# One kernel for an adaLN block: the first batch, the last batch and the written order changed

## The reference

```python
mod = (silu(c) @ wmod).reshape(16, 6, 1, 128)          # sa, ca, ga, sb, cb, gb
ga, gb = (2*(g >= 0) - 1) * maximum(abs(g), 0.25)      # for g = ga, gb
h = layernorm(x) * (1 + ca) + sa
x = x + ga * attn(h)
h = layernorm(x) * (1 + cb) + sb
x = x + gb * moe(h)

# attn: q, k, v = h @ W.T + b, 16 heads of 8
q = softmax(q, channels of a head); k = softmax(k, tokens)
state = k^T v (per head);  o = q state
o = (o - mean) * rsqrt(var + eps) * ln_g + ln_b;  return o @ Wo.T + bo

# moe: 8 experts, top 2 of softmax(h @ router_w), weights not renormalised
y = sum_e prob_e * (gelu(h @ w_in[e] + b_in[e]) @ w_out[e] + b_out[e])
```

## Time and profile before

| | us |
|---|---|
| median of 3 runs | 373.28 (373.12 to 373.51) |
| the profiled execution | 374.83 |
| its span on the core | 373.0 |

### The profile page before, as it was taken

How to read it: one execution, slowest core, us unless ns; L and a number is a source line. 1 busy time by engine, 2 the same in 40 slices (tenths; PEclk the granted TensorE clock), 3 DMA queues, 4 the chain that set the end, 5 groups by cost and what they waited for, 6 DMA issues and landing times.

```text
span 373.0 us, 8255 instructions
## 1 busy us (share of the span) xinstructions
PE 354.6 (95%) x2532; PEld 321.6 (86%) x2532; DVE 287.4 (77%) x1060; ACT 306.3 (82%) x524; POOL 227.8 (61%) x221
## 2 busy tenths in 40 slices
PE   2987999999999999999999999999999999999995
PEld 2766878899999989999999889999999989987984
DVE  3798888987897867787896888888886968656652
ACT  3567898999899899899998999899978968885740
POOL 3256947495649766583838658494758856184561
PEclk9999999999999999999999999999999999999999
DMA  5156055352607152241607035350606060416390
GB/s 171 32 147 228 0 167 203 116 173 47 223 20 228 55 181 105 114 168 52 236 3 255 31 114 171 113 173 25 232 5 226 2 206 24 175 54 175 141 304 36
DMA packets 18962, 47.84 MB, mean 128 GB/s; under 512 B 2587, under 2 KB 6118, under 8 KB 18662
## 3 DMA queue, kind: packets, MB, share of 16 engines
q1 hardware_dynamic: 18432, 46.77, 38.0%
...
## 4 chain that ended last, share of the span: by engine, by line
PE 69%; issue 8%; DVE 6%; ACT 6%; DMA 5%; POOL 4%; SPq 0%; ACTq 0%; POOLq 0%; DVEq 0%
PE pY L1042 22%; PE pH L1026 6%; PE pH L1028 6%; PE pH L1027 6%; PE pQV L990 3%; DMA gate_bc<-route_scratch 3%; PE pC L976 3%; PE pC L997 2%; PE pB L1012 2%; PE pQV L952 2%; PE pQV L968 2%; PE pQV L954 2%; PE pQV L953 2%; DMA wmod_sb<-in_L_wmod 2%; POOL v L421 2%
## 5 line engine op out<-in xcount | busy, mean ns | idle before, releaser
L1042 PE MATMUL pY<-wout,v 128*128 128x128 f32 x1024 | 130.8, 277 | 0.5 <-DVE v L1506 0.4
L1042 PEld LDWEIGHTS pY<-wout,v 128*128 128x128 f32 x1024 | 124.6, 192 | 5.0 <-DVE v L1506 1.2
L738 ACT ACTIVATE u<-pH,cols 128x512 f32<-128x512 f32 x128 | 85.3, 685 | 17.3 <-PE pH L1028 11.8
L421 POOL TENSOR_TENSOR v<-u,gate_bc 128x512 f32<-128x512 f32 x48 | 69.3, 1450 | 20.3 <-PE pY L1042 12.0
L1506 DVE TENSOR_TENSOR v<-u,gate_bc 128x512 f32<-128x512 f32 x80 | 61.8, 782 | 11.2 <-DMA gate_bc<-route_scratch 6.5
L1026 PE MATMUL pH<-h_hi,win_hi 128*128 128x512 f32 x128 | 59.1, 462 | 1.0 <-ACT u L738 1.0
L1027 PE MATMUL pH<-h_hi,win_lo 128*128 128x512 f32 x128 | 50.6, 395 | 0.0
L1028 PE MATMUL pH<-h_lo,win_hi 128*128 128x512 f32 x128 | 50.5, 394 | 0.0
L431 POOL TENSOR_TENSOR h_lo<-h,h_hi 128x512 fp32r<-128x512 f32 x16 | 20.4, 1278 | 35.5 <-ACT h_hi L666 35.4
L425 POOL TENSOR_TENSOR x_all<-x_all,yg 128x512 f32<-128x512 f32 x16 | 21.7, 1354 | 22.5 <-DVE yg L1513 15.5
L738 ACT ACT_TABLE_LOAD x27 | 34.6, 1283 | 0.5
...
## 6 DMA issues: line engine op xcount, KB each, us to landing
...
x_all<-in_L_attn_x SPq DMA_DIRECT2D x16, 256.0 KB, 5.0
out<-x_all SPq DMA_DIRECT2D x16, 256.0 KB, 2.3
...
route_scratch<-gateT SPq DMA_DIRECT2D x64, 4.0 KB
...
```

What stands on the lines that cost most here:

```text
L421: pool.tensor_tensor(v[:, e % U, :], u[:, e % U, :], gate_bc[:, b % 2, e, :], ALU.mult).then_inc(s["vp_done"], 1)
L738: act.activation(u[:, e % U, :], pH[:, e % 2, :], ACT.Gelu_apprx_tanh, bias=cols[:, e:e + 1]).then_inc(s["gelu_done"], 1)
L1042: i = mm(pY[:, t * P:(t + 1) * P], v[:, e % U, t * P:(t + 1) * P], wout[:, e, :], start=False, stop=(e == NE - 1), skip_group_check=True)
```

## The change

It has four parts.

1. **First loads.** wmod and all four weights are issued by SP right behind x of batch 0; the q and v biases come behind x1 and x2, and the experts and x3 ahead of the gates. ACT issues only c, runs silu, and issues the rows and bo (with a semaphore of its own, `bo_loaded`) after it.
2. **Batch 0.** PE does ten filler matmuls on ident while it waits, turns silu between them, and does modulation, then rows, then weights. ACT normalises two sub-tiles of batch 0 and DVE the other two; the second pair is turned into pQV, and DVE writes that half of h and h_hi from there while ACT writes the first half. DVE makes h_lo of batch 0. `gained_weight`, `centring` and `gain_centred` move behind kT(0) and qv(0).
3. **Last batch.** `finish_last` on DVE does the gating and the second residual of batch 15 in halves; SP stores the first half, ACT the second.
4. **The written order** of all engines changes in the first batches (on POOL in nearly all) and in the last three. `step(b)` is unchanged on every engine.

The diff, cut to its core:

```diff
@@ sync
             load_x(0)
-            for j, wt in ((0, Wq), (1, Wv)):
+            sp.dma_start(wmod_sb[:, :, :], wmod.rearrange("k (j c) -> k j c", j=NMOD)).then_inc(s["wmod_loaded"], DMA)
+            for j, wt in ((0, Wq), (1, Wv), (2, Wk), (3, Wo)):
                 sp.dma_start(w_nat[:, j, :], wt).then_inc(s["w_loaded"], DMA)
...
             load_x(2)
+            load_bias()
+            load_experts()
+            load_x(3)
             store_mod_gates()
-            load_x(3)
             spread_first_gates()
-            load_experts()
             load_expert_bias()
...
+            def store_first_half():
+                sp.wait_ge(s["out_last"], 1)
+                sp.dma_start(out_v[NB - 1][:, 0:NTOK // 2], x_all[:, NB - 1, 0:T // 2, :]).then_inc(s["stored"], DMA)
@@ gpsimd
             def rstd_L(n):
                 pool.wait_ge(s["ve1_done"], 2 * (n + 1))
-                w(pool, "xn1_ready", T * n)
+                w(pool, "xn1_ready", T * n - T // 2)
+                if n == 1:
+                    pool.wait_ge(s["xn1_half"], T // 2)
...
+            rstd_L(0)
+            rstd_L(1)
             masks()
-            rstd_L(0)
-            h_low(0)
...
@@ scalar
             act.dma_start(c_sb[:, :], c).then_inc(s["c_loaded"], DMA)
...
+            act.wait_ge(s["c_loaded"], DMA)
+            act.activation(silu_c[:, :], c_sb[:, :], ACT.Silu).then_inc(s["silu_ready"], 1)
             act.dma_start(rows[0:NE, :], b_in).then_inc(s["rows_loaded"], DMA)
...
+            def h_evac_first():
+                act.wait_ge(s["hT_done"], 1)
+                act.wait_ge(s["prep_mod"], 4)
+                half = slice(0, NTOK // 2)
+                act.activation(h_hi[:, half], pA[:, half], ACT.Identity, bias=modT[:, 0, 1:2], scale=modT[:, 0, 0:1])
+                act.activation(h[:, half], pA[:, half], ACT.Identity, bias=modT[:, 0, 1:2], scale=modT[:, 0, 0:1]).then_inc(s["hhi_ready"], 1)
...
+            act.wait_ge(s["out_last"], 2)
+            act.dma_start(out_v[NB - 1][:, NTOK // 2:NTOK], x_all[:, NB - 1, T // 2:T, :]).then_inc(s["stored"], DMA)
@@ tensor
+            pe.wait_ge(s["const_ready"], 1)
+            for _ in range(6):
+                mm(pH[:, 1, 0:P], ident[:, :], ident[:, :], start=True, stop=True)
+            pe.wait_ge(s["silu_ready"], 1)
+            pe.transpose(pH[:, 0, 0:NB], silu_c[:, :], ident[0:NB, 0:NB]).then_inc(s["tr_silu"], 1)
+            for _ in range(4):
+                mm(pH[:, 1, 0:P], ident[:, :], ident[:, :], start=True, stop=True)
...
+            def hT_first():
+                pe.wait_ge(s["xn1_ready"], T // 2)
+                for t in range(T // 2):
+                    pe.transpose(pA[:, t * P:(t + 1) * P], xn1[:, t, :], ident[:, :])
+                pe.wait_ge(s["xn1_half"], T // 2)
+                for t in range(T // 2, T):
+                    i = pe.transpose(pQV_flat[:, (t + 2) * P:(t + 3) * P], xn1[:, t, :], ident[:, :])
+                i.then_inc(s["hT_done"], 1)
...
+            modulation()
+            turn_rows()
             turn_weights()
-            modulation()
-            hT(0)
-            gain_centred()
+            hT_first()
             residual_gates()
+            keep_clock()
...
@@ vector
+            def ln1_apply_first():
+                dve.wait_ge(s["nmr1_ready"], 1)
+                for t in range(T // 2, T):
+                    dve.tensor_scalar(xn1[:, t, :], x_all[:, 0, t, :], rstd1[:, t:t + 1], nmr1[:, t:t + 1], ALU.mult, ALU.add).then_inc(s["xn1_half"], 1)
+
+            def h_evac_half():
+                dve.wait_ge(s["hT_done"], 1)
+                dve.wait_ge(s["prep_mod"], 4)
+                half = slice(NTOK // 2, NTOK)
+                dve.tensor_scalar(h_hi[:, half], pQV_flat[:, 4 * P:6 * P], modT[:, 0, 0:1], modT[:, 0, 1:2], ALU.mult, ALU.add).then_inc(s["h_half"], 1)
...
+            def h_low_first():
+                dve.wait_ge(s["h_half"], 2)
+                dve.wait_ge(s["hhi_ready"], 1)
+                dve.tensor_tensor(h_lo[:, :], h[:, :], h_hi[:, :].bitcast(F32), ALU.subtract).then_inc(s["hlo_ready"], 1)
...
+            def finish_last():
+                dve.wait_ge(s["mm2_done"], NE * NB)
+                w(dve, "out_ready", NB - 1)
+                b, halves = NB - 1, (slice(0, T // 2), slice(T // 2, T))
+                for hs in halves:
+                    dve.tensor_tensor(yg[:, hs, :], pY[:, :].rearrange("p (t c) -> p t c", t=T)[:, hs, :],
+                                      gb_bc[:, b, :].unsqueeze(1).to_broadcast([P, T // 2, P]), ALU.mult).then_inc(s["yg_last"], 1)
+                for j, hs in enumerate(halves):
+                    dve.wait_ge(s["yg_last"], j + 1)
+                    dve.tensor_tensor(x_all[:, b, hs, :], x_all[:, b, hs, :], yg[:, hs, :], ALU.add).then_inc(s["out_last"], 1)
...
             ln1_stats(0)
+            silu_turned()
             ln1_var(0)
+            ln1_apply_first()
+            modulation_columns()
             columns()
-            centring()
+            ln1_stats(1)
             attention_low()
+            h_evac_half()
...
```

More of the change, by code:

```diff
@@ L1582, in _ @@
-            out_var(0)
-            k_inv(1)
-            ln1_var(3)
-            q_bias(1)
-            v_bias(1)
-            q_max(1)
-            q_shift(1)
-            residual1(0)
-            q_sum(1)
-            ln2_stats(0)
+            residual1(0)
+            q_bias(1)
+            ln2_stats(0)
+            q_max(1)
+            ln2_var(0)
+            q_shift(1)
+            v_bias(1)
+            ln1_var(3)
+            q_sum(1)
+            k_inv(1)
             q_inv(1)
-            ln2_var(0)
+            state_out(1)
@@ L1610, in _ @@
             ln2_stats(1)
-            q_inv(2)
+            q_norm(2)
             ln2_var(1)
-            q_norm(2)
             gates_turned(0)
-            expert_bias()
+            ln1_stats(4)
+            weigh(0, 0)
+            ln1_var(4)
             k_max(3)
+            weigh(0, 2)
+            q_bias(3)
+            q_max(3)
             out_var(2)
-            weigh(0, 0)
-            q_bias(3)
-            weigh(0, 2)
+            v_bias(3)
+            route(1)
+            q_shift(3)
@@ L1621, in _ @@
             residual1(2)
-            route(1)
-            q_max(3)
-            k_inv(3)
             weigh(0, 4)
-            v_bias(3)
-            q_shift(3)
             gates_out(1)
             ln2_stats(2)
+            ln1_stats(5)
+            weigh(0, 6)
+            ln2_var(2)
+            k_inv(3)
+            weigh(0, 7)
+            ln1_var(5)
             state_out(3)
-            weigh(0, 6)
             q_sum(3)
-            ln2_var(2)
             q_inv(3)
             q_norm(3)
-            weigh(0, 7)
+            y_gated(0)
@@ L1637, in _ @@
             gates_turned(1)
-            ln1_stats(5)
-            ln1_var(5)
-            y_gated(0)
+            weigh(1, 0)
             k_max(4)
+            q_bias(4)
             out_var(3)
-            weigh(1, 0)
+            q_max(4)
             weigh(1, 2)
-            q_bias(4)
+            route(2)
             v_bias(4)
-            q_max(4)
-            route(2)
             q_shift(4)
+            residual1(3)
             weigh(1, 4)
-            residual1(3)
-            k_inv(4)
@@ L1663, in _ @@
             ln1_var(6)
-            gates_turned(2)
             y_gated(1)
+            k_max(5)
             weigh(2, 0)
+            q_bias(5)
+            v_bias(5)
+            out_var(4)
             weigh(2, 2)
-            k_max(5)
-            q_bias(5)
-            out_var(4)
             route(3)
-            v_bias(5)
             q_max(5)
+            weigh(2, 4)
+            q_shift(5)
+            residual1(4)
             gates_out(3)
-            q_shift(5)
-            weigh(2, 4)
@@ L1692, in _ @@
             weigh(3, 0)
+            weigh(3, 2)
             q_bias(6)
             q_max(6)
-            k_max(6)
-            v_bias(6)
-            q_shift(6)
-            weigh(3, 2)
-            route(4)
-            k_inv(6)
-            residual1(5)
-            gates_out(4)
-            weigh(3, 4)
-            ln2_stats(5)
+            route(4)
+            residual1(5)
+            ln2_stats(5)
+            q_shift(6)
+            weigh(3, 4)
+            gates_out(4)
+            weigh(3, 6)
```

538 lines of the change are left out of this document (271 added, 267 removed).

## The result

| | median us | ratio to before (95%) |
|---|---|---|
| changed kernel, first measurement | 375.07 | 1.0043 [1.0029, 1.0058] |
| the same, second measurement (a1) | 375.58 | 1.0048 [1.0032, 1.0065] |

The kernel became slower by 0.4 to 0.5%, 1.6 to 1.8 us; 368.5 was forecast. The median of before lay between 373.3 and 374.1 over the jobs, so ratios are the safer comparison with it. The profiled executions hide most of the difference: after 374.92 (span 373.2), before 374.83, which is 1.6 above before's median.

What follows compares the result with a forecast made beforehand. TensorE has no gap in the middle (20.97 us per batch), so only head, ramp, waits and tail can earn: -2.1 - 1.4 - 0.7 - 0.6 = -4.8 us, median 368.5 from 373.28; 8-in-10 range 365.2 to 371.6.

Steps and rivals of the forecast that it cites:

- Head: Start up to the first real matmul: kT(0) at 12.8 instead of 14.85 us, -2.1 us, bounds -3.0 and +0.3.
- cold-clock rival: Head: fillers fail to raise TensorE's clock level before kT(0), the head's gain is gone, 370.6 us; chance 0.06.
- 13.0 with the slow: Head: kT(0)'s start if the four keep_clocks' 8 pieces run at the slow pitch; 12.2 with the fast.
- Ramp: First batches, reordered so batch 0 runs ahead: -1.4 us, bounds +1.5 and -4.0.
- -1.05: Ramp: further gain taken because batch 0's experts, ready earlier, fill PE's waits between 57 and 90 us.
- about 1.0 of PE's waits there is filled: Ramp, hidden(0,0) to combine(0,0): part of the sum that put combine(0,0) at 53.9, 3.25 us earlier.
- named bound of +1.5: Ramp's upper bound: batches 1 and 2, whose DVE work now comes later, meet PE again.
- Middle: Saturated batches: POOL's rows move among ten batches, but POOL idled 20.3 us before its weigh, so nothing.
- rival "slower": Middle: POOL's new order makes ACT and PE wait 0.65 us in each of ten batches, 375.0 us; chance 0.06.
- two signs that were to make the forecast wrong: Whole kernel: a pace over 21.2 us per batch, or combine(0,0) after 57 us.
- Drain: Last batches: rstd_o(15) behind the weighs brings elg 1.2 earlier, wait at gate_turn(14) goes; -0.7 us, bounds 0 and -1.8.
- Tail: After the last matmul: halves on DVE let the second store issue at 370.0 instead of 370.62, -0.6 us; landing 0.

Runs made afterwards that it cites:

- tail: Kernel before with only the last batch's gate product and addition in two halves on DVE, stored by SP and ACT: 373.24 us, ratio 0.9976.
- head: Changed kernel's loads, head and last batch in halves, every engine's list after the head in the order of before: 370.04 and 370.39 us.
- oldmid: Changed kernel with every list from y_gated(2), residual2(2) and combine(2,2) on in the order of before, last batch still in halves: 372.13 us.
- newlate: 'head' up to y_gated(2), residual2(2) and combine(2,2), every list from there in the changed kernel's order: 376.79 us, ratio 1.0081.
- act_bias: 'oldmid' with expert_bias()'s four 128x128 products into bout moved from DVE to ACT: 371.42 us, ratio 0.9934.
- r_bias2: 'oldmid' with DVE's expert_bias() back behind gates_turned(0) and TensorE's moe_bias(0) put right ahead of combine(0,0): 373.12 us, ratio 0.9982.
- m_dve: Changed kernel with only DVE's list for batches 3 to 5 in the order of before: 375.04 us, ratio 1.0051.
- m_res: Changed kernel with one GpSimd call moved, residual2(8) back ahead of rstd_L(13) from behind rstd_O(11): 375.43 us, ratio 1.0035.

## Why the prediction was wrong

Forecast and found, in us: head -2.1 and about -3.0 ('tail' to 'head'); tail -0.6 and -0.9 ('tail'); ramp -1.4 and +1.9 ('head' to 'oldmid'); middle 0 and drain -0.7, together +3.4 ('oldmid' to the changed kernel), of which 0.9 up to batch 5 and 2.5 behind it. -3.0 - 0.9 + 1.9 + 3.4 = +1.4, against 1.6 to 1.8 measured. Each kernel differs from the next by one piece, so these add up by construction: they say where the time lies, and 'newlate' shows that a piece can cost another amount in other company.

- **Head.** Right in mechanism, too small, with one length misread. Silu at 3.13 was exact. Rows and weights landed earlier than taken, and with the upper level from 5.8 us on the four turns of batch 0 were over by 8.6, not 10.1: kT(0) at 11.6, not 12.8. The cold-clock rival is real but belongs to single executions: the profiled ones of 'head' took 3.1 and 2.3 us more than its medians. Its mechanism was another, for kT(0) and qv(0) ran at the upper level in every trace (kT's second part starts 0.23 us before its third). The misread length is the four keep_clocks: "13.0 with the slow" pitch counts their eight pieces at 0.213 us, the pitch of 128 columns, but they have 256 columns and start 0.43 us apart at the lower level. So 10.1 + 1.2 + 3.4 gives 14.7, and the late traces have kT(0) at 14.6 to 14.8 (13.2 where the change came at 11.2). On the port DVE won: h_lo took its 0.68 us and rstd beside it 1.39. The row that the prediction sets beside the Trainium skill (SBUF — State Buffer, "Who interferes with whom"), ve with 0.87 us, has one SBUF input, not two as in the sentence cited; qn at 131 us (1.67 us) has two and is the better row for it, and the qn rows from 152 us on do not fit the sentence, if their order of starts is right.
- **Ramp, the first step that failed** (-1.4 forecast, +1.9 found). "Batch 0's experts being ready earlier gives PE something to do where it waited between 57 and 90" was argued and not read from a row, and the rows were there. The waits of TensorE in before's trace from 57 to 90 us are these two, 0.8 us together:

```profile
PE pH L1026 <- ACT u L738: 0.6, 1, 0.6
PE pY L1042 <- DVE v L1506: 0.2, 1, 0.2
```

  So there was hardly room for the -1.05. Nor for "about 1.0 of PE's waits there is filled" between hidden(0,0) and combine(0,0): before waited 0.5 us there, and the new order put its wait of 1.72 for residual1(1) into that stretch, which took 16.8 us where 15.0 were worked out. residual1(0) (27.04, forecast 27.5) and hidden(0,0) (38.2, forecast 38.9) came nearly as worked out, in part by luck: kT(0) was 1.2 earlier than forecast, and residual1(0) followed it in 15.45 us, not 14.7; combine(0,0) came at 55.0, not 53.9. Batches 1 and 2 pay for batch 0, as the named bound of +1.5 said. DVE's full list explains 0.7 of it ('act_bias'); the place of expert_bias none that 'r_bias2' could show. Which moves make the other 1.2 is open.
- **Middle, the second and larger.** "POOL has slack: nothing" took an average (20.3 us idle) for slack at each place. GpSimd's order acts through the operations of DVE that it lengthens (qn at 131 us, 1.67 us for 0.68) and through SP's queue (store_out ahead of a gate block, 248 us); both follow from where its operations fall, not from how busy it is. With 'm_dve' and 'm_res' each wait is gone from its place in the trace; of the 3.4 us neither shows a sure part at the end. The rival "slower" had the side and 375.0, but that number was luck: its mechanism was 0.65 us in every batch. The pace of the batches is unchanged (attend_project comes 20.96 to 21.00 us apart in six of the eight steps before the drain); it is a few single waits. So neither of the two signs that were to make the forecast wrong came, a pace over 21.2 or combine(0,0) after 57: single waits set off neither.
- **Drain.** Wrong sign. ACT's wait for weigh(13,1), 1.26 us in before, went as forecast, but ACT came to h2_evac(14) 1.2 us later (h at 328.50, before 327.27). So the router's table load came at 331.12, 0.15 earlier and not 1.2, gate_turn(14) waited 0.74 instead of 0.67, so the wait that was to go stayed, and TensorE stood 0.70 for h2T(15) instead of 0.28.
- **Tail.** Right, 0.9 for 0.6. The last store is issued 0.6 us sooner after yg, as worked out (1.45 us for 2.06), and 0.3 lies in the landing, which the sum took as 0. The last store of before, and the two halves of the changed kernel (DMA issues from 365 us on, columns as in the earlier trace rows):

```profile
out<-x_all SPq DMA_DIRECT2D x1, 256.0 KB, 2.0
...
out<-x_all SPq DMA_DIRECT2D x1, 128.0 KB, 1.7
out<-x_all ACTq DMA_DIRECT2D x1, 128.0 KB, 1.7
```

  The price that the prediction worked out from the Trainium skill (DMA: Bandwidth & Descriptors, "Anatomy of one DMA"), -0.9, was the better one: its saving of 0.3 us for 128 KB is what the rows show. Its fixed 2.0 us is not: that section is on DMAs that GpSimd issues, and here a whole store of 128 KB from SP or ACT took 1.7.
